# A perceiver block on one core: all token rows loaded and the first query weights split while cross-attention ends, and 48 transposes of the identity at the start

## What is computed

```python
x = x + xattn(_layernorm(x), ctx_1024, Wq, Wk, Wv, Wp, bp)        # 16 heads of 32, 1601 keys each
x = x + attn(_layernorm(x), Wq, bq, Wk, bk, Wv, bv, Wo, bo)       # scores + alibi bias, softmax, 64 keys
x = x + ffn(_layernorm(x), W_fc, W_proj)                          # relu squared, then 5 steps of a spiking neuron
```

## Time and profile before

| | us |
|---|---|
| median of 3 runs | 1852.61 (1852.07 to 1852.99) |
| the profiled execution, whole | 1856.79 |
| its span | 1855.0 |
| PE busy | 1819.4 |
| DVE busy | 1142.1 |
| POOL busy | 907.5 |
| ACT busy | 842.3 |
| mean granted TensorE clock | 0.995 |

### The profile page before, as it was taken

How to read it: one execution, slowest core, us unless ns; L and a number is a source line. 1 busy time by engine, 2 the same in 40 slices (tenths; PEclk the granted TensorE clock), 3 DMA queues, 4 the chain that set the end, 5 groups by cost and what they waited for, 6 DMA issues and landing times. The chain is left out here.

```text
span 1855.0 us, 65510 instructions
## 1 busy us (share of the span) xinstructions
PE 1819.4 (98%) x28940; PEld 1586.9 (86%) x28940; DVE 1142.1 (62%) x1366; ACT 842.3 (45%) x1046; POOL 907.5 (49%) x830
## 2 busy tenths in 40 slices
PE   7999999999999999999999999999999998999998
PEld 6878898989898989898989898988888876777887
DVE  5554848484748475757566565757484757574265
ACT  4534545454545454544444454545453523344332
POOL 0234737383838382828373646455564644435111
PEclk9999999999999999999999999999999998999999
DMA  6310202020202020202020201111020222033110
GB/s 225 132 53 2 82 3 82 3 81 3 81 4 81 3 82 3 81 4 81 3 81 4 81 15 70 42 42 64 21 82 2 74 95 72 25 92 102 46 57 24
DMA packets 43373, 101.18 MB, mean 55 GB/s; under 512 B 19136, under 2 KB 20672, under 8 KB 42976
## 3 DMA queue, kind: packets, MB, share of 16 engines
q1 hardware_dynamic: 43104, 96.88, 14.9%
HBM read 86.48 MB, written 8.29 MB: 51 GB/s over the span
## 5 line engine op out<-in xcount | busy, mean ns | idle before, releaser
L540 POOL TENSOR_TENSOR fold<-fold,prob 128x256 f32<-128x256 f32 (+1 forms) x704 | 725.0, 1030 | 55.2
L111 PE MATMUL ring<-y_parts,w_keep 128*128 128x402 f32 (+1 forms) x3072 | 610.0, 352 | 1.4 <-PEq L187 1.4
L111 PEld LDWEIGHTS ring<-y_parts,w_keep 128*128 128x128 f32 x3072 | 554.6, 189 | 15.3 <-issue 1.8
L111 PE MATMUL ring<-wv_s,y_parts 128*128 128x512 f32 x2304 | 552.1, 396 | 0.0
L111 PEld LDWEIGHTS ring<-wv_s,y_parts 128*128 128x128 f32 x2304 | 427.7, 188 | 95.4
L534 POOL TENSOR_TENSOR fold<-prob 128x256 f32<-128x256 f32 x64 | 69.1, 1079 | 655.0 <-ACT prob L592 655.0
L557 ACT ACTIVATE k_sb<-ring 128x402 f32<-128x402 f32 (+1 forms) x256 | 129.4, 506 | 364.9 <-PE ring L111 364.9
L735 DVE TENSOR_TENSOR prob<-prob,peak_rows 128x1024 f32<-128x1024 f32 (+1 forms) x192 | 277.7, 1499 | 11.8 <-ACT peak_rows L588 11.8
L582 ACT ACTIVATE prob<-s_ps 128x1536 f32<-128x1536 f32 (+1 forms) x128 | 200.0, 1562 | 133.9 <-PE s_ps L883 133.9
L592 ACT ACTIVATE prob<-prob 128x1024 f32<-128x1024 f32 (+1 forms) x192 | 207.4, 1123 | 2.9 <-DVE prob L735 2.9
L883 PEld LDWEIGHTS s_ps<-q_sb,k_sb 32*64 32x64 f32 x13312 | 156.0, 130 | 29.9 <-issue 29.9
(11 more groups left out here) (208 smaller groups left out, 1576.1 us busy)
## 6 DMA issues: line engine op xcount, KB each, us to landing
y_raw<-yT SPq DMA_DIRECT2D x48, 804.0 KB, 7.3
y_raw<-yT SPq DMA_DIRECT2D x16, 792.0 KB, 9.9
f_raw<-w_ffn SPq DMA_DIRECT2D x22, 512.0 KB, 3.5
v_sb<-y_left SPq DMA_DIRECT2D x1, 2304.0 KB, 10.3
v_sb<-v_left SPq DMA_DIRECT2D x16, 130.0 KB
p_x<-x SPq DMA_DIRECT2D x4, 512.0 KB, 6.5
q_scratch<-p_x SPq DMA_DIRECT2D x8, 256.0 KB, 2.0
q_sb<-q_scratch SPq DMA_DIRECT2D x16, 128.0 KB, 9.2
```

The source lines that it names most:

```text
L111: mm = pe.matmul(out, left(a, c), right(b, c), start=(c == 0 and n == 0), stop=(c == DC - 1 and n == 2))
L540: pool.tensor_tensor(acc[0:m], acc[0:m], prob[0:m, i, t, :], ALU.add).then_inc(sum_step, 1)
```

## The change

Four things, all in the code of one core:

- **Prologue:** PE gets 48 transposes of the identity (`WARM`) behind its wait for the identity, ahead of the first token rows. They write a PSUM bank that the fourth tile's rows overwrite later.
- **Batch 0:** DVE's three `left_low` stand behind `peaks` and the first half of `largest` of block 2, no longer ahead of them.
- **End of cross-attention:** SP loads the self-attention's query weights into `w_late`, which shares its memory with the value weights `wv_s`, once all value products are done, and token rows 3 to 7, once the third `gather` is. It waits for the rows before the block ends. ACT and DVE split the query weights there. `gather(2)` stands ahead of `output(0)`. POOL adds the bias to five rows there, not three.
- **Start of the self-attention block:** rows and query weights are no longer loaded; POOL adds the bias to three rows at once; DVE's `attention_weights(0)` is gone, and so is the add of tile 4 between the parts of `dve_norm`; the banks are dealt anew, so that the fourth turned tile goes to `s_ps` and not to `ring`, and product 5 to `s_ps` bank 1; the waits follow that.

```diff
-ROWS_AHEAD = 3
+ROWS_AHEAD, BIASED = 3, 5
...
+        with ExitStack() as late:
+            self.w_late = late.enter_context(nc.sbuf_tensor("w_late", [P, DC, D], F32))
...
             pe.wait_ge(ident_ok, 2)
+            for n in range(WARM):
+                pe.transpose(t_ps[3][:, n % DC * P:(n % DC + 1) * P], ident[:], ident[:])
             turn(0)
...
+            sp.wait_ge(full, UNITS * B)
+            sp.dma_start(sh.w_late[:], awq.rearrange("(c p) e -> p c e", p=P)).then_inc(aw_in, 16)
+            sp.wait_ge(out_lo, len(BY_QUARTER))
+            sp.dma_start(x_rows[:, ROWS_AHEAD:], x[ROWS_AHEAD * P:].rearrange("(t p) d -> p t d", p=P)
+                         ).then_inc(x_late, 16)
+            sp.wait_ge(x_late, 16)
...
+            act.wait_ge(aw_in, 16)
+            act.activation(y.w_side[0][:, 0], sh.w_late[:], ACT.Copy).then_inc(aw_hi, 1)
             act.wait_ge(o_out, NBLK * B)
...
+            gather(2)
             output(B - 1, 0, last_bank(0), q_sb[:, 0, :])
-            gather(2)
+            dve.wait_ge(aw_hi, 1)
+            dve.tensor_tensor(y.w_side[0][:, 1], sh.w_late[:], y.w_side[0][:, 0].bitcast(F32), ALU.subtract)
...
-            rows(0, ROWS_AHEAD, HALF)
-            sp.dma_start(w_raw[0], attn_w[0].rearrange("(c p) e -> p c e", p=P)).then_inc(aw_in[0], 16)
-            rows(1, HALF, TT)
+            sp.dma_start(bo_row, bo.rearrange("(a d) -> a d", a=1).broadcast_to((P, D))).then_inc(bo_in, 16)
...
             co.dve_add(dve, range(HALF))
-            co.dve_norm(dve, 0, range(HALF, HALF + 1))
-            attention_weights(0)
+            co.dve_norm(dve, 0)
             co.dve_low(dve, range(HALF))
-            co.dve_add(dve, range(HALF + 1, TT))
+            co.dve_add(dve, range(HALF, TT))
...
             def qk(u):
                 half, n, i = qk_unit(u)
-                pe.wait_ge(aw_lo, n + 1)
+                reached(pe, aw_lo, n)
                 pe.wait_ge(co.lo_ok, HALF * (half + 1))
-                if u < 4:
-                    pe.wait_ge(co.added, HALF + u + (u > 0))
+                if u == 0:
+                    pass
+                elif u < 4:
+                    pe.wait_ge(co.added, HALF + u + 1)
```

More of the change, by code:

```diff
@@ L545, in _ @@
             pool.wait_ge(x_in, 32)
-            for t in range(ROWS_AHEAD):
-                pool.tensor_tensor(y.w_raw[:, t, :], y.w_raw[:, t, :], y.w_raw[:, ROWS_AHEAD, :], ALU.add)
+            for t in range(BIASED):
+                if t == ROWS_AHEAD:
+                    pool.wait_ge(x_late, 16)
+                rows = y.w_raw if t < ROWS_AHEAD else x_rows
+                pool.tensor_tensor(rows[:, t, :], rows[:, t, :], y.w_raw[:, ROWS_AHEAD, :], ALU.add)
         @block.scalar
@@ L769, in keys_phase @@
                     largest(b, i, 0)
+                    if not past and i == 2:
+                        for j in range(LEFT_SLOTS):
+                            left_low(j)
                     subtract(b, i - 1)
@@ L773, in keys_phase @@
                         output(b - 1, i + 1)
-                    elif i == 1:
-                        for j in range(LEFT_SLOTS):
-                            left_low(j)
                 if not past:
@@ L1081, in dve_add, with dve_norm @@
             self.n += 1
-    def dve_norm(self, dve, half, between=()):
+    def dve_norm(self, dve, half):
         mv, ve, step = self.mv, self.ve, self.step
@@ L1214, in qk_bank @@
         def qk_bank(u):
-            return wide[(u + 3) % 4] if u < 8 else t_bank if u == 9 else ring
+            return wide[u % 4] if u < 8 else t_bank if u == 9 else ring
         def v_bank(t):
@@ L1304, in divide @@
                                    ALU.mult).then_inc(pr_ok, 1)
-            for t in range(ROWS_AHEAD, TT):
-                pool.wait_ge(x_in[t // HALF], 16)
-                pool.tensor_tensor(x_sb[:, t, :], x_sb[:, t, :], bp_row, ALU.add).then_inc(co.biased, 1)
+            for t in range(BIASED, TT):
+                pool.tensor_tensor(co.xn[:, t, :], co.xn[:, t, :], bp_row, ALU.add).then_inc(co.biased, 1)
             pool.wait_ge(bo_in, 16)
@@ L1785, in _ @@
             cross_out(range(AHEAD_OUT, TT - 1))
-            co.pe_turn(pe, range(HALF - 1))
-            pe.wait_ge(co.added, AHEAD_OUT + 1)
-            co.pe_turn(pe, range(HALF - 1, HALF))
+            co.pe_turn(pe, range(HALF))
             cross_out(range(TT - 1, TT))
```

43 lines of the change are left out of this document (20 added, 23 removed).

## The result

| | before | changed |
|---|---|---|
| median | 1852.8 (1852.07 to 1856.01, 4 runs) | 1842.87 (1841.61 to 1845.33, 4 runs) |
| ratio, 95% interval | | 0.9939, 0.9927 to 0.9950 |
| profiled execution, whole | 1856.79 | 1845.33 |
| its span | 1855.0 | 1843.4 |

The kernel became 9.9 us faster by the medians, 11.5 by the two profiled executions; 13.0 were forecast. Against the forecast of 1839.6 the median is 3.3 us higher, just within the range, which ends at 1843.0. Run a second time on another chip, the changed kernel gave 1841.07 (1840.48 to 1842.89, 5 runs) beside 1855.16 for the kernel before: 0.9922 (0.9909 to 0.9936). The forecast as a ratio, 1839.6 / 1852.6 = 0.9930, lies between the two.

A forecast was written before the change was run, and what follows sets the result against it. PE was busy 1819.4 of 1855.0 us, so time could be won only from its idle or low-clock stretches. Terms 3.5 - 0.5 + 0 + 10.0 = 13.0 us took the median from 1852.6 to 1839.6; range 1837.0 to 1843.0.

The forecast's parts named there:

- Part 1: Prologue: 48 warm-up transposes raise PE's clock early; first key product at 38.3, not 41.84; gain 3.5 us.
- late warm-up: Prologue rival: 48 transposes at low clock end at 12.5, delaying first tiles; gain 1.5 or less, 1841.6; chance 0.12.
- Part 2: Batch 0, left-over rows: 2.6 us gained by PE are given back waiting for a split; 0.5 us lost.
- the rival happened: Batch 0 rival: PE's new 3 us pause brings the clock down; 1.7 us more lost, 1841.3; chance 0.13.
- Against it: there the pause was followed by small score matmuls: Batch 0: argument that the clock stays up, since the new pause lies between dense matmuls; otherwise 1.7 us more lost.
- If the pause is gone, so is the low clock behind it: Batch 0: removing PE's 1.30 us wait for the peaks also removes the low clock after it, 1.7 us.
- Part 3: End of cross-attention: added loads, splits and additions lie beside PE's last work and end before the border; cost 0.
- Part 4: Start of last block: first query product at 1534.4 instead of 1545.01, keys at 1548.0 instead of 1557.99; gain 10.0 us.
- what held PE: Last block rival: DVE's short steps and the clock, not the rows, set 1545.01; only about 6 us, 1843.6; chance 0.07.
- Slower at the border: Border rival: SP's wait for the five rows delays the block; landing at 1532.7 eats 13 us, from 1856; chance 0.01.

The follow-up runs named there:

- e1: Kernel before with only the 48 warm-up transposes added: 1849.16, ratio 0.9973.
- e11: The changed kernel run again unchanged, on another chip: 1841.07, ratio 0.9922.
- e4: Changed kernel plus 14 bridging transposes before the queries, and batch 0's three splits between the peaks and the maxima: 1870.13, ratio 1.0094.
- e8: Like e4, but warm-up of six 512-column fp32 matmuls and one as bridge, 28 instructions more than the kernel before: 1843.23, ratio 0.9929.
- e9: Like e4, but warm-up of two large fp32 matmuls and 30 transposes, one matmul as bridge, 72 instructions more than the kernel before: 1840.95, ratio 0.9925.
- e10: e8 with the five rows' load held back until the second last weighing has ended: 1839.77, ratio 0.9918.
- e2: Kernel before with only the move of batch 0's three left-over splits: 1855.99, ratio 1.0006.
- e3: Changed kernel without the warm-up transposes and with batch 0's splits at their old place: 1848.36, ratio 0.9969.
- e7: Kernel before with only the early load and split of the query weights: 1849.90, ratio 0.9969.
- e6: Kernel before with only the five token rows loaded early, POOL's additions and DVE's new order: 1852.32, ratio 0.9985.
- e5: Kernel before with 62 transposes at the start and nothing else, 124 instructions more: 1881.34, ratio 1.0134.

## Why the prediction was right or wrong

- **Part 1, gain 3.5: the mechanism right, the size a matter of the clock.** In e1 and e11 the first key product came at 38.34 and 38.37, as told (38.3). In the first profile only 1.4 came. The warm-up itself was early enough (the 48 transposes took 6.8 to 8.4 us, 8.4 told), so the rival "late warm-up" is not what happened; PE's wait for the weights behind the 16 transposes was. The prediction's own steps imply that wait (16 transposes from 10.0 end near 11.9, the queries start at 13.1), but it took the clock as safe once it was up. The clock fell behind 1.80 us here, not behind 1.40 (e11) or 1.03 (e1); with work in the pause (e4, e8, e9, e10) it stayed up each time. Without the warm-up the same product comes at 39.6 to 41.8, so the 3.5 is the upper end of 1.2 to 3.5.
- **Part 2, loss 0.5: the trade right, the rival happened.** In e2 PE came 2.6 us earlier, as told, then waited 2.06 us, not 3.0, for the very split that was named; and the clock fell, 1.6 us. By e2 the edit loses 1.4 against the profile before, and 2.9 against e3 and e7. Two steps failed. "Against it: there the pause was followed by small score matmuls": the clock fell before dense ones as well. And "If the pause is gone, so is the low clock behind it", 1.7 us, took for a steady cost what came in one of six executions with that pause.
- **What was not seen: 3.2 us in batch 0.** The issue pause at 57.4 and the low clock behind it are absent in every kernel with transposes or large matmuls in front, 28 to 124 instructions more. That they move a piece's end fits, but e8 shows that the count alone is not the whole cause. With part 2's loss of 1.4 and about 0.3 elsewhere, the measured 2.1 follows. It hid that the first profile's prologue fell short. The step that failed is to read PE's pauses only at the places that the diff touches, and to cost added instructions by their run time alone.
- **Part 3, cost 0: wrong.** All transfers and all work beside PE landed in time, as told: SP's wait and the border did not come later for them. But the rows' load stood in front of PE's own next piece of instructions: 0.8 us in the changed kernel and 1.4 in e11, 4.6 in e3, 6.1 in e6, and gone but for 0.4 in e10. The nearest row for what a load costs is the load's own landing; who else uses the DMA engines was not asked.
- **Part 4, gain 10.0: the steps right.** 10.1 between the two profiles, by the steps told: first query 14.43 after the start (14.4 told), keys 27.9 (28.0). DVE's normalising began 7.28 us into the block (7.2 told). Rows and weights alone bring 6.8 and 6.4 us of it at the keys, so neither alone was what held PE: each was late behind the other. In e1, e2 and e5 the old block took 1.2 to 2.5 us less than in the profile before, so against them the gain is 7.6 to 8.9.
- **The rivals.** "Slower at the border" had the right place but the wrong queue: what was late was PE's instructions, not the rows. Its last figure is also loose: rows that land at 1532.7 would eat the 13 us and give 1852.6; 1856 would take another 3.4 us.
- **One execution as the price list.** Every term was priced on a profile that lay 4.18 us above its kernel's median, and the sum was then taken from that median. Three stretches were at or near their slow end in it.

For the whole: of 13.0 us told, 11.6 came in the first profile and 14.2 in e11's, so that the median fell within the range is in part luck: an unforeseen gain of 3.2 stood against losses that were not told. By term, 13.0 would have been 3.5 (or 1.4 when the clock falls) + 3.2 - 1.4 - 0.8 to 1.4 + 10.1 less up to 1.2 for uneven turns.

## What to carry to other kernels

Cost added instructions not only by their time but by what they move: compare PE's "issue" pauses over the whole time line before and after, above all behind a loop's jump and where hundreds of short matmuls run; 28 instructions more or less can shift such a pause, and the same work in fewer, larger matmuls shifts it less. A prefetch that has time to spare should start when PE is in long matmuls, not when it needs its next instructions soon. Work that moves from a waiting engine to the next can come back as that one's wait: e2 gained 2.6 us and paid 3.9. Price a change on more than one execution: the same code took up to 2.5 us less in a stretch of 38 us.

## What the runs showed of the hardware

- Instructions came in packets of 16 KB, 256 instructions each, through the DMA engines that move the data; that the packets in question were PE's is inferred. Behind a queued load of 1.25 MB such a piece came so late that PE stood still for 1.8 to 3.2 us (e3, e6, e8, e9), or 0.3 to 0.9 us where its end lay nearer the weighing's start (the changed kernel, e4, e11). Right behind a loop's jump it paused 1.2 to 2.1 us in each of 13 turns, with the DMA queues empty of data (e4, e5): 62 transposes of the identity, 9.96 us of work that delayed the real ones by 1.3 us, made the kernel 26 us slower.
- The length of a pause alone did not tell here whether the clock falls. It fell behind 1.30 us (before, at 87.5), and not behind 1.25 to 1.27 at the same place in e1, e3, e5, e6 and e7. It fell behind the issue pause of batch 0 with 1.64 to 1.71 us (before, e2, e3, e7), not with 1.43 (e6); behind the waits of 2.04 to 2.06 us in batch 0 (changed, e2, e11) and behind all pauses of 2.66 us and more. It stayed up behind 1.40 (e11) and 1.81 us (e9, in the weighing), and of the 26 pauses of 1.2 to 2.1 us in the loops of e4 and e5 only four brought it down. The same kernel's first key product came at 40.41 in one execution and at 38.37 in another. The Trainium skill (TensorE: Matmul & The Clock Gate, What's actually happening) has it that the chip's look at activity runs freely and doesn't start with the kernel; these differences between runs agree. With one fp32 matmul of 512 columns (1.02 us on PE) in the prologue's pause the clock stayed up in e8, e9 and e10.
